# Three unused tensors shift SBUF addresses so that fp32r matmul operands lie 64 bytes apart in 128

## What is computed

```python
# layer 0: 8-head attention, softmax masked by adj, then 4 hops
for _ in range(4): z = 0.9 * einsum(pros, z) + 0.1 * vh
x = layernorm(x + z)
# layer 1: one head of width 256, masked softmax, output weight Wo
x = layernorm(x + softmax(mask(Q K^T / 16)) @ V @ Wo + bo)
# layer 2: 8 heads with output weight Wo
x = layernorm(x + attention(x) @ Wo + bo)
# layer 3: per edge label d: mean over neighbours with adj == d, then a gated update
out = relu(concat_d(weight_d @ x) @ Wd.T + bd)
r = sigmoid(out @ Wri.T + x @ Wrh.T + b); z = sigmoid(out @ Wzi.T + x @ Wzh.T + b)
n = tanh(out @ Wni.T + bni + r * (x @ Wnh.T + bnh))
x = layernorm((1 - z) * n + z * x)
```

## The kernel before

| product | before: starts | apart | after: starts | apart |
|---|---|---|---|---|
| x with weights (L393, L405, L612) | x 32, w 0 | 32 | x 64, w 0 | 64 |
| o with weights (L393) | o 64, w 0 | 64 | o 64, w 0 | 64 |
| z2 with weight wo2 (L583) | z2 0, w 0 | 0 | z2 64, w 0 | 64 |
| mask with xw (L622) | wT 64, xw 64 | 0 | wT 0, xw 64 | 64 |

## Time and profile before

### The profile page before, as it was taken

How to read it: one execution, slowest core, us unless ns; L and a number is a source line. 1 busy time by engine, 2 the same in 40 slices (tenths; PEclk the granted TensorE clock), 3 DMA queues, 4 the chain that set the end, 5 groups by cost and what they waited for, 6 DMA issues and landing times.

```text
span 1647.7 us, 44214 instructions
## 1 busy us (share of the span) xinstructions
PE 1560.3 (95%) x17168; PEld 1420.7 (86%) x17168; DVE 1313.7 (80%) x3133; ACT 1223.1 (74%) x4074; POOL 718.3 (44%) x710
## 2 busy tenths in 40 slices
PE   6778999999999999999999999999999999999885
PEld 5677998999999989999998999999899999998764
DVE  3566888888888888888888888888888888888753
ACT  4577777777878777787877778877777787777642
POOL 1344444444454444445444453544445354544311
PEclk9799999999999999999999999999999999999997
DMA  5100011110011111001111100011110001100000
GB/s 195 33 11 28 27 33 34 34 30 27 11 34 33 34 34 34 24 12 34 33 34 34 33 24 20 25 33 33 34 34 24 25 19 34 33 27 15 14 7 13
DMA packets 71424, 51.62 MB, mean 31 GB/s; under 512 B 4400, under 2 KB 69936, under 8 KB 70576
## 3 DMA queue, kind: packets, MB, share of 16 engines
q1 hardware_dynamic: 71216, 48.79, 9.9%
HBM read 40.39 MB, written 8.39 MB: 30 GB/s over the span
## 4 chain that ended last, share of the span: by engine, by line
PE 74%; ACT 18%; DVE 4%; issue 2%; POOL 1%; DMA 0%; SPq 0%; POOLq 0%; DVEq 0%; ACTq 0%
PE bank_A L393 14%; PE bank_B L393 8%; PE bank_B L612 6%; PE bank_C L393 5%; PE bank_A L437 5%; ACT E L685 5%; ACT E L747 5%; PE bank_B L437 4%; PE bank_A L612 3%; PE bank_A L411 3%; PE bank_B L405 3%; PE bank_A L423 2%; PE bank_X L533 2%; PE bank_X L544 2%; PE bank_A L508 2%
## 5 line engine op out<-in xcount | busy, mean ns | idle before, releaser
L828 POOL TENSOR_TENSOR E<-E,rsum 128x512 f32<-128x512 f32 x256 | 269.5, 1059 | 438.3 <-DVE rsum L922 301.3
L836 POOL TENSOR_TENSOR rstd<-var,minus_half 128x2 f32<-128x2 f32 x128 | 100.6, 786 | 210.8 <-DVE var L967 210.7
L816 POOL TENSOR_SCALAR absent<-absent 128x256 int32<-128x256 int32 x64 | 55.4, 866 | 247.3 <-DMA absent<-in_adj 247.3
L974 DVE TENSOR_SCALAR y<-y,mv,rstd 128x256 f32<-128x256 f32 x192 | 125.5, 694 | 31.4 <-POOL rstd L836 31.4
L733 ACT ACTIVATE kT<-bank_B,col 128x256 f32<-128x256 f32 x64 | 26.9, 472 | 111.3 <-PE bank_B L393 111.3
L915 DVE COPY_PREDICATED_SCALAR bank_A<-absent,fill 128x512 f32 x128 | 92.3, 743 | 17.4 <-PE bank_B L423 16.2
L393 PE MATMUL bank_A<-xT_hi,w_hi 128*128 128x256 f32 x384 | 102.5, 289 | 0.0
L393 PE MATMUL bank_A<-xT_hi,w_lo 128*128 128x256 f32 x384 | 99.5, 281 | 0.0
L685 ACT ACTIVATE E<-bank_A,nmax 128x128 f32<-128x128 f32 x256 | 91.4, 388 | 9.7 <-DVE nmax L918 9.7
L685 ACT ACTIVATE E<-bank_B,nmax 128x128 f32<-128x128 f32 x256 | 94.7, 441 | 0.0
L431 PE MATMUL bank_C<-ident,E 128*128 128x128 f32 x512 | 80.0, 280 | 14.6 <-POOL E L828 13.8
(11 more groups left out here) (223 smaller groups left out, 6402.8 us busy)
## 6 DMA issues: line engine op xcount, KB each, us to landing
xt_in<-in_xt SPq DMA_DIRECT2D x64, 128.0 KB, 2.6
absent<-in_adj SPq DMA_DIRECT2D x64, 128.0 KB, 2.9
x_in<-in_x SPq DMA_DIRECT2D x32, 256.0 KB, 3.4
out<-y SPq DMA_DIRECT2D x32, 256.0 KB, 2.2
adj<-in_adj SPq DMA_DIRECT2D x32, 128.0 KB, 2.4
adjT<-in_adjt SPq DMA_DIRECT2D x32, 128.0 KB, 2.2
stage<-in_weights SPq DMA_DIRECT2D x3, 1024.0 KB, 9.3
row<-in_rows SPq DMA_DIRECT2D x1, 1024.0 KB, 8.2
```

Source lines behind the costliest of these rows:

```text
L828: nc.gpsimd.tensor_tensor(e, e, rs[:, part].unsqueeze(2).to_broadcast([P, SB, P]), ALU.mult).then_inc(e_sig.sem, 1)
L836: nc.gpsimd.tensor_tensor(rstd[part][:], var[part][:], minus_half[:], ALU.pow)\
L974: a = nc.vector.tensor_scalar(y[part][:, g, :], src[g], mv[part][:, g, 0:1], rstd[part][:, g:g + 1], ALU.subtract, ALU.mult)
```

## The change

Three unused tensors are allocated among the others. The first replaces an unused tensor of 64 bytes per partition by one of 128; the second (64 bytes) stands before `xw`; the third (160 bytes) before the `xT_hi` tensors. No instruction, wait or shape differs; only addresses do.

```diff
-        sb("gap", [P, 16])
+
+        sb("gap_0", [P, 32])
 
         x_in = sb("x_in", [P, G, D])
@@
         wT = [sb(f"wT_{u}", [P, G, LABELS, P], F32R) for u in range(2)]
+        sb("gap_1", [P, 16])
         xw = sb("xw", [P, 8 * D])
@@
         xn = [sb(f"xn{L}", [P, G, D]) for L in range(2)]
+        sb("gap_2", [P, 40])
         xT_hi = [sb(f"xT_hi{L}", [P, NC, GN], F32R) for L in range(4)]
```

## The result

The changed kernel takes 1640.1 us, the median of 11 runs (1632.71 to 1642.36), where the kernel before took 1647.01 us on the same chip (11 runs, 1642.51 to 1650.09): a ratio of 0.9949, with an interval of 0.9936 to 0.9963. The ratio makes it faster by 0.51%, 8.4 us, and the two medians differ by 6.9 us; 2.1 us was forecast. The profiled execution took 1636.13 us, with a span of 1634.3. All lines after the change stand 3 higher (L393 is L396, L405 is L408, L612 is L615, L622 is L625, L583 is L586, L533 is L536).

A forecast was written before the change was run, and what follows sets the result against it. TensorE was taken to set the pace, with ACT on the path for 8.7 us of each 47.80 us period. The terms summed to -0.065 us per period, 2.1 us over 32 rounds, giving 1645.0 us; 8-in-10 range 1639.5 to 1650.0.

The forecast's parts named there:

- the middle case: Whole kernel: the time stays within 0.3% of before, chance 0.69.
- 64 apart: Pricing of each fp32r family at the new distance by o's matmuls, 118 ns each, assuming swapped sides make no difference.
- the last rival: The change doesn't do what it says: the address period may be other than 128, leaving x unpriced; no chance given.
- Project on x: 84 project matmuls on the path, 118 ns before and after: 0.02 us gained per period.
- Natural: 12 natural matmuls on the path (v2), 1.45 becomes 1.42: 0.03 us gained per period.
- lab: 18 matmuls of 512 columns on the path, 1 ns gained each: 0.02 us per period.
- wo2: 12 matmuls on the path leaving 0 apart, six taking 0.71 us against 0.70 and 0.71: 0.01 us lost.
- agg: 8 mask-with-xw matmuls on the path, four taking 0.47 against 0.48 us: 0.005 us gained.
- 6. and 7.: Moved fp32 matmuls, and ACT, DVE, POOL and DMA accesses to moved tensors: all priced at nothing.
- No address effect: Rival: apparent distance differences come from a step's form or place; time 1647.1 us, chance 0.20.
- Slower: Rival: 64 is bad with x, z2 or mask stationary; 0.40 us per period, 12.7 us, 1659.8; chance 0.13.
- Faster: Rival: streams at one distance lose 3 ns per matmul; 15.6 us, 1631.5 if complete, 1639 at half; chance 0.17.

The follow-up runs named there:

- x64: Kernel before with 32 unused bytes ahead of xT_hi, moving x to 192 bytes past the weights: 1640.98 against 1647.19 us, ratio 0.9959.
- x64m256: Changed kernel with 128 bytes more ahead of xT_hi, so x is at 64 instead of 192 modulo 256: 1644.78 us against before's 1647.59, ratio 0.9984.
- rest64: Changed kernel without its x part: x stays at 160, o, z2, masks and fp32 tensors move; 1651.02 us against before's 1647.19, ratio 1.0014.
- micro: Separate small kernel, other engines idle: fp32r matmul bursts at 16 operand distances, three entries each for 256 columns; pitch 113 to 120 ns for 256 columns.
- x0: Kernel before with 96 bytes ahead of xT_hi, x at 0 bytes from the weights: 1650.99 against 1647.19 us, ratio 1.0021.
- micro2: Small kernel like micro: streams of 18 at nine distances, each behind a first matmul of 128 to 240 columns; at 192 all eight entries settled at 113 ns.
- xo192: Kernel before with 128 bytes ahead of xw and 160 ahead of xT_hi, x and o both at 192: 1638.16 against 1650.71 us, ratio 0.9932.
- micro3: micro2 with its stationary tensor 16 bytes on, six distances: 119.3 to 120.0 ns at 112, all entries 113.3 at 192.

## Why the prediction was wrong

That a distance of addresses is read from the pitch, that the gain lies on PE's path, and that its sign is a gain held. The size failed: 8.4 us against 2.1, and the middle case (within 0.3%), which I had given most of the chance, did not come. The median, 1640.1, lies just inside the range of 1639.5 to 1650.0, below the 1641 to which the forecast's own bounds went.

**The step that failed** is the pricing of "64 apart", by the row of o, ahead of steps 1 to 5, with the inference that "swapping moving and stationary side makes no difference at 64". The period is 256 bytes. o lay at 64 and x comes to lie at 192 and, for natural and lab, at 64 from the other side. The row of o could not price that place, which no row of before holds: o has a steady 118 ns, while at 192 the steps k2 and q2 ran at 113 in 12 of 25 periods, and z ended at 113 in 24. x64 shows that this place alone carries the gain (0.9959), x64m256 that 64 modulo 256 does not give it (0.9984). I had written this down as the last rival ("modulo 256 x would come to lie at 192 from the weights where o now lies at 64") and then sent it to "one of the cases above" instead of giving it a price.

Step by step:

1. Project on x. 0.02 us per period forecast. Measured in the first period of after: 0.16 us in k0, q0, k2 and q2 and 0.11 in z, which is half x and half o; in the second 0.03 in the four and 0.05 in z. The term of the sum was mis-sized because it took the pitch at 192 for that of o at 64, and because it assumed one pitch per place, while the trace has 113 and 118 at the same one. Nor could the recorded lengths have told: project's went from 281 to 280 ns while k2 and q2 went from 118 to 113 in half of the periods. Also, the 84 matmuls were too many: nh and rh do not count, as rest64 shows.
2. Natural. 0.03 forecast as 1.45 to 1.42; measured 1.36 and, in the other period, 1.41. The direction was right; the size was a third of what the first period has, from the same cause.
3. lab. 0.02 forecast for the three parts; 1.37 to 1.39 instead of 1.40, 0.04 us for two of them and 0.01 for the third: the right direction and twice the size. micro has 228.9 ns for 64 apart and 233.3 for 96, so my lower bound (a loss by twice o's pitch) was wrong: 512 columns have an order of their own.
4. wo2. 0.01 lost forecast; 0.71 and 0.71 measured against 0.70 and 0.71: right. The mean pitch went from 116.3 to 117.9.
5. agg. 0.005 forecast; its first part stays at 0.48 in the chain, its mean pitch goes from 119 to 118 ns: right within the trace.
6. and 7. fp32, ACT, DVE, POOL and DMA at nothing: right. Transposes stay at 0.44 and exponentials at 1.40, and the fp32r steps hold 0.40 of the 0.42 us.

**How the bound was read.** I put ri, ni, nh and rh on the path because the chain of waits runs over them. It does, but only because no wait is recorded where PE meets ACT; z starts 8.12 to 8.15 us after L533 whatever PE does before it. Of the 170 fp32r matmuls that I counted per period 48 have no worth. It cost the forecast little, but would have cost much had I forecast a larger gain for o.

**The rivals.** "No address effect" fell with micro. It is also how I had read "SBUF — State Buffer", section "Who interferes with whom", of the Trainium skill, which gives PE one read port for the moving operand and an independent one for weight loads and lets it wait for no one. No run here tests whether PE waits for other engines, which were idle in micro. But that the two reads are independent does not carry over to the address: one matmul takes 113 to 120 ns by the distance of the two and the entry. "Slower" did not come: natural at 64 ran at 118 or 113 ns and not at 126. That another place can cost time is shown by x0, at 0 apart: 1.0021. "Faster" named an effect of the right kind, that o loses its 118 once its neighbours lie well, and z does show it; but the 3 ns per matmul that it counted was no level that exists. The level is 5 ns lower, held by some of the matmuls only. That half of its price, 1639, lies near the measured 1640.1 is luck.

**Signs.** Of those I named, v2 at 1.42, project at 1.42 and 47.73 us from L533 to L533 are refuted in the first period, and v2 and project nearly hold in the second. "If project goes under 1.40, the faster one" was the right sign to watch.

**What stays open.** Which event decides the rhythm at each step in the whole kernel: micro2 shows that the moment of entry can, and xo192 that what lies around matters, but no run changes one and holds the other. Why xo192 has k2, q2 and v2 in the fast rhythm in every period and the change in half of them. What in the hardware has a period of 256 bytes. And how much of the differences lies in the first and last periods, where not all layers are there: the span of after, 1634.3 us, is shorter than the 1636.0 of xo192, though its periods are longer (47.52 against 47.42), and the medians say the opposite of the spans. The single executions of one kernel differ by up to 10 us (1632.71 to 1642.36 for the changed one). A part of this is the clock: it is 1.00 through the middle of the traces (152 to 1579 us of after) and changes between its two levels, 1.2 and 2.4 GHz, at both ends, and there the executions differ. Of the changed kernel the fastest has a mean granted clock of 0.984 and the slowest 0.978, and the profiled executions of after and xo192 have 0.982 and 0.978.

## What to carry to other kernels

For streams of fp32r matmuls with a weight load each, try the moving operand 192 bytes (modulo 256) after the stationary one; it costs an unused tensor. It makes 113 ns instead of 118 to 120 for 256 columns likelier and doesn't ensure it: behind a short matmul all 16 streams came to 113, after a wait and behind wide ones two streams of 24 did not, and in the whole kernel it depended on the step and the period. Count in the timeline how many of the streams have it. Price such an effect by starts in the timeline and a small kernel at each candidate distance, not by the length of a matmul or by one row of another tensor, and ask first for the period of the effect. Before counting a gain on a step of the chain of waits, look at what the next meeting point with another engine needs, and whether its distance from the start of the period changes when the step does: that no wait is recorded there does not prove that the step sets the pace.

## What the runs showed of the hardware that I had not expected

- The pitch of fp32r matmuls of 256 columns depends on the distance of the two operands in SBUF, modulo 256 bytes: from 113 ns (192) to 120 ns (0 and 96). For 512 columns it is 228 ns (0) to 235 ns (160), in another order.
- There are two stable rhythms at 64 and 192, 113 and 118 ns. Behind one short matmul 4 entries of 16 found the fast one at 64 (micro2 and micro3) and 16 of 16 at 192; in micro it was none of three and one of three. In the whole kernel steps change between them from one period to the next, so that two periods with the same work take 47.38 and 47.56 us.
- Besides the distance, the start within 32 bytes counts: at 112, with the moving side alone off the multiple of 32, the streams came to 113 ns; with the stationary side alone off it, to 120.
- fp32 transposes of 128 columns have 109 ns in micro and take 0.44 us for four before and after; ACT's copies of 512 columns from bank C have means of 634 to 639 ns in all the kernels, and its eight exponentials take 1.39 to 1.40 us.
- A wait can stand in no row: z of the kernel before waits some 0.1 us for ACT, without idle time of PE in the trace.
- "TensorE: Matmul & The Clock Gate", section "Back-to-back issue gap", of the Trainium skill gives N/2.4 + 2.5 ns for a matmul by itself, an estimate of 109 ns for 256 columns and of 216 for 512. The best streams here are 4 and 12 ns above it, at 113 and 228.
